# A four-layer decoder on one core: the k transfers issued by ScalarE, together with new stretch heads, half-wise waits, two-row moves of the maxima and new scheduler figures

## The reference

```python
q, k, v = x @ Wq + bq, kv @ Wk + bk, kv @ Wv + bv          # split in 16 heads of 8
w = softmax(q @ k.T * scale + mask, axis=-1)               # 512 x 512 or 512 x 77
y = layernorm(x + (w @ v) @ Wo + bo)
```

## Time and profile before

| what | value |
|---|---|
| median of 3 runs | 2757.01 us (2756.97 to 2764.75) |
| the profiled execution's own time | 2757.16 us |
| its span, first to last instruction | 2755.4 us |
| mean granted TensorE clock | 0.846 of full speed |
| first segment, first to last instruction | about 40 to 1104 us |
| second segment | about 1214 to 1790 us |
| third segment (L3c) | about 2291 to 2447 us |

### The profile page before, as it was taken

One profiled execution on the slowest core, in us unless ns is written; L12 is line 12 of the kernel. 1 busy time (PEld: TensorE's weight loads), 2 busy tenths in 40 slices (PEclk: granted clock), 3 DMA queues, 4 the chain that ended last, 5 costly groups with the idle time before them and its releaser, 6 DMA issues. The chain is left out here.

```text
span 2755.4 us, 44085 instructions
## 1 busy us (share of the span) xinstructions
PE 2173.7 (79%) x15402; PEld 1094.6 (40%) x15402; DVE 1629.0 (59%) x3578; ACT 1194.6 (43%) x2185; POOL 654.1 (24%) x845
## 2 busy tenths in 40 slices
PE   2699999975899996658999988629687773768888
PEld 1133355433233342634554444228422221335556
DVE  4588766577777732455676545235567772436666
ACT  0277756642267753223666675304232211433332
POOL 4211111134201110432121112044236673100000
PEclk9699999976589997777999998659888875779998
DMA  3300011100101010521111000038400001111111
GB/s 116 114 25 25 27 36 38 29 15 23 35 25 27 17 27 1 172 89 50 35 30 37 20 20 17 12 102 298 149 0 1 0 1 25 30 47 54 54 62 47
DMA packets 106846, 133.01 MB, mean 48 GB/s; under 512 B 26006, under 2 KB 90326, under 8 KB 105987
## 3 DMA queue, kind: packets, MB, share of 16 engines
q1 hardware_dynamic: 101556, 115.32, 14.0%
q0 software_dynamic: 3776, 7.79, 0.8%
q10 hardware_dynamic: 1296, 7.08, 0.7%
HBM read 70.65 MB, written 13.49 MB: 31 GB/s over the span
## 5 line engine op out<-in xcount | busy, mean ns | idle before, releaser
L1326 ACT ACTIVATE probs<-psE 128x512 f32<-128x512 f32 (+2 forms) x1248 | 698.0, 584 | 405.7 <-PE psE L1165 229.4
L1450 DVE TENSOR_REDUCE maxima<-psM 128x2 f32<-128x1024 f32 (+4 forms) x640 | 678.9, 1082 | 312.7 <-PE psM L1142 142.7
L1165 PE MATMUL psE<-q_stack,k_stack 53*128 53x512 bf16 (+3 forms) x1152 | 372.1, 361 | 36.6 <-ACT probs L1326 26.3
L1142 PE MATMUL psM<-k_stack,q_stack 51*128 51x512 bf16 (+3 forms) x1280 | 358.9, 352 | 32.2 <-DVE maxima L1450 13.9
L1601 POOL TENSOR_SCALAR pool_t<-mean_var 128x4 f32<-128x4 f32 x60 | 15.0, 250 | 935.7 <-DVE mean_var L1387 931.0
L2299 DVE SCALAR_TENSOR_TENSOR hres<-psM,gates,hres 128x128 f32<-128x128 f32 x512 | 144.2, 345 | 81.8 <-PE psM L2233 81.0
L1165 PEld LDWEIGHTS psE<-q_stack,k_stack 53*128 53x128 bf16 x1152 | 98.2, 94 | 229.2 <-ACT probs L1326 144.8
L1142 PEld LDWEIGHTS psM<-k_stack,q_stack 51*128 51x128 bf16 x1280 | 101.5, 96 | 196.2 <-issue 105.6
L1077 PE MATMUL psM<-masks_bf,ident_bf 64*128 64x128 bf16 (+2 forms) x832 | 148.3, 260 | 16.7 <-DMA k_stack<-k_parts 15.8
L2233 PEld LDWEIGHTS psM<-values,probs 128*128 128x128 f32 x1024 | 136.5, 195 | 59.4 <-issue 58.9
L1185 PE MATMUL psB<-probs,values 128*32 128x256 f32 (+3 forms) x1712 | 154.3, 432 | 2.4 <-ACT probs L1326 1.0
(11 more groups left out here) (411 smaller groups left out, 3614.4 us busy)
## 6 DMA issues: line engine op xcount, KB each, us to landing
q_stack<-q_parts SPq DMA_DIRECT2D x432, 64.0 KB
values<-experts_dram SPq DMA_DIRECT2D x40, 514.0 KB, 4.7
values<-experts_dram SPq DMA_DIRECT2D x32, 512.0 KB, 3.2
k_stack<-k_parts SPq DMA_DIRECT2D x192, 64.0 KB
hid<-experts_dram SPq DMA_DIRECT2D x15, 514.0 KB, 4.4
work<-experts_dram SPq DMA_DIRECT2D x15, 514.0 KB, 4.7
pack<-pack_dram SPq DMA_DIRECT2D x1, 4647.0 KB
work<-sorted SPq DMA_DIRECT2D x70, 65.0 KB, 3.7
```

The costliest lines, as they stand in the source:

```text
L1142: out, len(heads), keys, lo, max_mask(c, t), lambda i, to, start, stop: nc.tensor.matmul(to, q_stack[lo:lo + R_MAX, job.a % Q_SLOTS, pair_ ...
L1165: lambda h, to, start, stop: nc.tensor.matmul(to, ks[lo:lo + R_END, pairs[h], k * P:k * P + c.kn], q_stack[lo:lo + R_END, job.a % Q_SLOTS, ...
L1326: nc.scalar.activation(probs[0:c.kn, m % 2, heads[0]:heads[-1] + 1, q0:S], psE[0:c.kn, n % 2, 0:len(heads) * (S - q0)].rearrange("p (h q) ...
L1450: nc.vector.tensor_reduce(top, psM[:, at:at + len(banks), 0:per * keys].rearrange("p b (h k) -> p b h k", h=per), AX_X, ALU.max, negate=Tr ...
```

## The change

1. **Who issues k.** The 12 `k_move` transfers of every attention (and the bias rows of L2c) are issued from ScalarE's queue, in the order that the plan gives, between its exponentials and copies. q and the rows of maxima stay with SP.
2. **Halves.** The transfers go half by half: first the six of half 0, then the six of half 1, each half with semaphores of its own. A wide attention's sets 0 and 1 wait for half 0 alone, sets 2 and 3 for half 1. A narrow one still waits for both.
3. **Stretch heads.** For jobs marked `ahead` (L0a, L1a and L2s of sequence 0, L3c of all four) `k_split` runs on DVE instead of POOL.
4. **Rows of maxima.** The two bfloat16 parts lie together in `max_parts`, so one transfer writes both rows of a half: one issue for a wide set (two before), two for a narrow set (four before).
5. **Quantization.** The DVE task `quant_b` is cut in two, `quant_b` and `quant_c`, so that other work can be placed between; `peak` has one buffer for each sequence.
6. **Scheduler figures.** An issue is assumed to take 0.65 us of SP's or ACT's time (1.3 us for the two of a narrow set's rows) and to land 1.8 us after it; most DVE post-processing tasks are assumed a little shorter. With that the order on every engine changes.

The core of the diff (names of the places between @@ are added):

```diff
@@ Plan @@
             self.put(t + 8.0, "quant_b", job)
+            self.put(t + 12.0, "quant_c", job)
...
-            self.moved[n % 2] += 32 if c.wide else 64
+            self.moved[n % 2] += 16 if c.wide else 32
...
-            return [("q_move", m.job, 2 * NB - 1), ("k_move", m.job, 2 * NB - 1)] if m.g == 0 else []
+            if m.g not in (0, 2):
+                return []
+            last = NB - 1 if m.job.att.wide and m.g == 0 else 2 * NB - 1
+            return [("q_move", m.job, last), ("k_move", m.job, last)]
...
-        if task in ("q_move", "k_move"):
+        if task == "k_move":
+            return ("ACT",)
+        if task == "k_split":
+            return ("DVE",) if x.ahead else ("POOL",)
+        if task == "q_move":
...
-                    "quant_b": 9.5, "post_c": 1.75}[task]
+            return {"post_a": {"norm": 1.6, "mlp": 3.1}.get(x.post, 2.4) if task == "post_a" else 0.0,
+                    "post_b": {"twice": 2.8, "tail": 5.0}.get(x.post, 1.4) if task == "post_b" else 0.0,
+                    "q_evac": 0.8, "rq_evac": 2.3, "rk_evac": 2.3, "split": 0.5, "share": 0.7, "mix": 0.7, "quant_a": 1.7,
+                    "quant_b": 3.6, "quant_c": 4.0, "post_c": 1.4, "k_split": 2.2 if task != "k_split" or x.att.wide else 1.0}[task]
...
-            elif engine == "SP":
-                moves = task in ("q_move", "k_move")
-                n = 1 if moves else 2 if x.job.att.wide else 4
-                free[engine] = at + 0.06 * n
-                queue = max(queue, free[engine]) + (0.1 if not moves else 0.35 if task == "q_move" or x.att.wide else 0.08)
-                end = queue + 1.7
+            elif engine == "SP" or task == "k_move":
+                free[engine] = at + (1.3 if task == "rows_evac" and not x.job.att.wide else 0.65)
+                ended["ISSUED", item] = free[engine]
+                end = free[engine] + 1.8
...
@@ segment @@
+        def parts(me, engine, src, tmp, out, n):
+
+            me.mark(engine.tensor_copy(out[:, 0, 0:n], src[:, 0:n]))
+            me.wait()
+            me.mark(engine.tensor_tensor(tmp[:, 0:n], src[:, 0:n], out[:, 0, 0:n], ALU.subtract))
+            me.wait()
+            me.mark(engine.tensor_copy(out[:, 1, 0:n], tmp[:, 0:n]))
+            me.wait()
+            return engine.tensor_tensor(out[:, 2, 0:n], tmp[:, 0:n], out[:, 1, 0:n], ALU.subtract)
...
+                def wait_k_split(eng, job):
+
+                    if job.ahead:
+                        eng.wait_ge(k_split_ahead, split_no["k_split_ahead"][job])
+                    else:
+                        eng.wait_ge(k_split, split_no["k_split"][job])
+
+                def part_rows(j, hb):
+                    return slice(64 * hb + j, 64 * hb + NB * (DH - 1) + j + 1, NB)
+
+                def move_k(eng, job, i):
+
+                    hb, j = divmod(i, NB)
+                    nk = job.att.nk
+                    ks, _ = k_side(job)
+                    if i == 0:
+                        wait_k_split(eng, job)
+                        if before_k[job]:
+                            eng.wait_ge(exp_taken, job_exps(before_k[job]))
+                    if j == 0 and job in bias_rows:
+                        at = 64 * hb + R_BIAS
+                        src = job.att.bias if bias_rows[job] else zeros_bf[:, 0:nk]
+                        eng.dma_start(ks[at:at + 3, :, 0:nk], src.unsqueeze(1).to_broadcast([3, H // 2, nk]))\
+                            .then_inc(k_moved(job, hb), 16)
+                    eng.dma_start(ks[part_rows(j, hb), :, 0:nk],
+                                  k_parts[64 * hb:64 * hb + 64, (0, 1, 2, 0, 1, 0)[j], 0:nk])\
+                        .then_inc(k_moved(job, hb), 16)
...
-                            if m.g == 0 and step == 0 and b == 0:
-                                pe.wait_ge(q_moved[job.a % Q_SLOTS], q_need[job])
-                                pe.wait_ge(k_moved(job), k_need[job])
+                            if m.g in (0, 2) and step == 0 and b == 0:
+                                for hb in (m.g // 2,) if c.wide else (0, 1):
+                                    pe.wait_ge(q_moved[job.a % Q_SLOTS][hb], q_need[job])
+                                    pe.wait_ge(k_moved(job, hb), k_need[job])
...
@@ scalar queue @@
-                            since(act, k_split, evac_no["k_evac"][job] - 1)
+                            if job.a:
+                                wait_k_split(act, atts[job.a - 1])
...
+                        elif task == "k_move":
+                            move_k(act, job, item[2])
...
@@ vector queue @@
+                        elif task == "k_split":
+                            if job.att.rope:
+                                dve.wait_ge(k_roped, k_roped_no[job])
+                            else:
+                                wait_freed(dve, job, "k")
+                            if job.a:
+                                for hb in range(2):
+                                    dve.wait_ge(k_moved(atts[job.a - 1], hb), k_need[atts[job.a - 1]])
+                            splits += 1
+                            parts(me, nc.vector, k_full, q_tmp, k_parts, job.att.nk).then_inc(k_split_ahead, 1)
...
-                            high, low = max_parts[:, m.n % 2, :, 0:heads], max_parts[:, m.n % 2, :, heads:2 * heads]
-                            top = maxima[:, m.n % 2, :, 0:heads]
+                            n = min(heads, 8)
+                            split = max_parts[:, m.n % 2, :, 0:2 * heads].rearrange("p t (b two h) -> p t b two h", two=2, h=n)
+                            high, low = split[:, :, :, 0, :], split[:, :, :, 1, :]
+                            top = maxima[:, m.n % 2, :, 0:heads].rearrange("p t (b h) -> p t b h", h=n)
...
-                            quantize(me, u)
+                            quant_scale(me, u)
+                        elif task == "quant_c":
+                            quant_round(me, job.u)
...
@@ sync queue @@
-                            j, hb = divmod(i, 2)
-                            if i == 0:
+                            hb, j = divmod(item[2], NB)
+                            if item[2] == 0:
...
-                        elif task == "k_move":
-                            i, nk = item[2], job.att.nk
...
-                            for part in range(2):
-                                for hb in ((m.g // 2,) if c.wide else (0, 1)):
-                                    lo, p0 = 64 * hb + R_MAX + part, pair_of(HG * m.g) if c.wide else 0
-                                    n = min(heads, 8)
-                                    at = heads * part + (0 if c.wide else 8 * hb)
-                                    sp.dma_start(q_stack[lo:lo + 1, m.job.a % Q_SLOTS, p0:p0 + n, :],
-                                                 max_rows[at:at + n, m.n % 2, :]).then_inc(rows_moved[m.n % 2], 16)
-
-        def quantize(me, u):
+                            for hb in ((m.g // 2,) if c.wide else (0, 1)):
+                                lo, p0 = 64 * hb + R_MAX, pair_of(HG * m.g) if c.wide else 0
+                                at = 0 if c.wide else 16 * hb
+                                sp.dma_start(q_stack[lo:lo + 2, m.job.a % Q_SLOTS, p0:p0 + n, :],
+                                             max_rows[at:at + 2 * n, m.n % 2, :]).then_inc(rows_moved[m.n % 2], 16)
...
@@ segments @@
-            Job("att", u, L0a, "std", xt[:, u]),
+            Job("att", u, L0a, "std", xt[:, u], ahead=u == 0),
...
-            Job("att", u, L1a, "std", xt[:, u]),
+            Job("att", u, L1a, "std", xt[:, u], ahead=u == 0),
...
-            Job("att", u, L2s, "inner", yt[:, u], ("lnx_g", "lnx_b")),
+            Job("att", u, L2s, "inner", yt[:, u], ("lnx_g", "lnx_b"), ahead=u == 0),
...
-            Job("att", u, L3c, "std", xt[:, u]),
+            Job("att", u, L3c, "std", xt[:, u], ahead=True),
```

More of the change, by code:

```diff
@@ L425, in needs @@
             return [("root", x, 0)]
+        if task == "quant_c":
+            return [("quant_b", x)]
         if task == "post_b":
@@ L461, in engines @@
             return ("ACT",)
-        if task in ("q_evac", "rq_evac", "rk_evac", "split", "share", "mix", "quant_a", "quant_b", "post_a", "post_b",
+        if task in ("q_evac", "rq_evac", "rk_evac", "split", "share", "mix", "quant_a", "quant_b", "quant_c", "post_a", "post_b",
                     "post_c"):
@@ L1407, in _ @@
                     nc.vector.memset(values[:, :, :, :, DH:DH + 1], 1.0)
+                    splits = 0
                     for item in plan.order["DVE"]:
@@ L1573, in _ @@
                             if q_before:
-                                pool.wait_ge(q_moved[q_before.a % Q_SLOTS], q_need[q_before])
+                                for hb in range(2):
+                                    pool.wait_ge(q_moved[q_before.a % Q_SLOTS][hb], q_need[q_before])
                                 pool.wait_ge(q_split, split_no["q_split"][job] - 1)
```

108 lines of the change are left out of this document (46 added, 62 removed).

## The result

The changed kernel takes 2881.5 us in the median of four runs (2866.2 to 2889.0), the kernel before 2757.0 us: 1.044 times as long, 95% interval 1.039 to 1.049. The forecast was 2708 us. The profiled execution after took 2866.2 us with a span of 2864.4.

The account below looks back on a forecast made before the run. TensorE was taken as the bound in the wide-attention stretches, VectorE from 552 to 690 us. The terms -11.5 - 12 - 5 - 26.5 - 4 + 10 = -49 us took 2757.2 to 2708 us, range 2670 to 2765.

Parts of the forecast that it names:

- What bounds the kernel: TensorE in the wide-attention stretches, 396.5 of 414 us and 264.2 of 275; VectorE leads from 552 to 690 us.
- ScalarE's price: Cost of moving k and bias issues to ScalarE: +10 us, between 0 and 100, most issues standing alone.
- first rival: ScalarE becomes the bound: overdue k transfers in a row stop exponentials and TensorE in wide attentions; 2798 us, chance 0.13.
- The upper bound: Twelve issues in a row: some 6 us of TensorE in each of 17 wide attentions, 100 us.
- The price of single issues: One issue between two exponentials on ScalarE costs some 0.1 us, nothing where ScalarE waits for TensorE.
- The heads: First score matmuls at stretch starts come sooner through halves and two queues: L0a -11.5 us, L2s -12.
- two queues are no faster: Rival: transfers themselves are the limit, so heads gain less and L3c's period nothing; 2743 us, chance 0.10.
- L3c: Last narrow attentions: head -10, first maxima rows -1.4, period from 28.5 to 21 to 26 us, -15; in all -26.5.
- The -10 of the head: L3c's first attention: q alone on SP lands at 2308.2 instead of 2318.3 us.
- Scheduler figures: New issue and duration figures, changing the order on every engine: 0 us, with -10 to +20.
- L1a: Sequence 0's head starts sooner, though VectorE is the bound there: -5 us, bounds 0 and -12.
- rows of maxima: Outside L3c, fewer issues per set shorten TensorE's waits for them: -4 us, 0 to -8.

Follow-up runs that it names:

- e13: e11 with its order kept, plus twelve small transfers nobody waits for, issued in a row from ScalarE in each wide attention; +229 us against 2675.9 us.
- e11: e1 with the old durations of VectorE's tasks and the new model of SP's queue; 2676 us.
- e1: The changed kernel with the k transfers of every attention issued from SP again, all else kept; 2693 us, ratio 0.976.
- e12: The changed kernel with k's transfers due no earlier than the planned end of the last exponential that reads their slot; 2754 us.
- e15: e11 plus twelve small transfers nobody waits for per wide attention, issued from ScalarE singly behind twelve successive exponentials; +23 us against 2675.9 us.
- e2: The kernel before with only the k transfers moved to ScalarE's queue, under the old model of transfers; 2777 us, ratio 1.009.
- e8: e1 with the split of k given back to GpSimd everywhere; 2709 us.
- e6: e1 with the old durations of VectorE's tasks and the old model of SP's queue; last stretch 460 us, whole time not stated.
- e3: The changed kernel with the planner allowing the next k transfer only 0.3 us after the last is issued; 2802 us.
- e17: e12 with e11's durations of VectorE's tasks; 2795 us.

## Why the prediction was wrong

**What bounds the kernel** was right: e13 stalls ScalarE, which is busy only 45% of e11's span, and the time follows because TensorE, in the wide stretches, goes idle.

**The step that failed** is ScalarE's price: "the plan may take a ready transfer in any such gap, so most will stand alone. [...] I take +10". 188 us were paid (e1). Two things in it were wrong.

First, the premise on the order. The prediction's own first rival named the condition, "where k's parts are late, the transfers are overdue and come in a row", and gave it 0.13. It is the slot that is late, not k's parts, and that could be read in the plan: with two slots k waits for the last exponential of the attention two before, while its due times lie earlier. e12 moves nothing but these and gets 128 us back.

Second, the price of a row. The upper bound was 6 us for each wide attention: 7.8 us of issues less two exponentials in flight. Measured by itself a row costs 11.5 us (e13). TensorE's idle time was bounded about rightly (6.7 us for each row); the clock was left out, which stood at its lower level for 9.7 us behind the row shown and costs 5.0 us for each. With 11.5 in place of 6 the rival's sum gives 2757 - 59 + 17 x 11.5 = 2894 us, near the 2881 measured. By the twelve wide rows that the trace has, they are 138 of the 188 us (an estimate from e13), which fits the 128 that e12 gets back; the rest are the rows of narrow attentions, single and short groups of issues, and the order, not separated.

The price of single issues was right: 0.1 us each was said, 0.1 measured (e15), 20 us for all issues of k (e2). (The count was 8 too high: the trace has 8 bias rows, 440 issues in all.)

**The heads** were right for TensorE's first scores. L0a -10.5 (forecast -11.5, at 66.0 us and not 65), L2s -11.3 (-12). Counted from the stretch's start L3c's first scores came 9.1 us sooner (-10). But the second queue gives only part of it. With all of k on SP (e1) the three still start 7.6, 7.9 and 4.0 us sooner than before, so the second queue adds 2.9, 3.4 and 5.1. In L0a and L2s that leaves most to the halves and the order of issues, since e8 shows nothing for the split; the two were not tested apart. Here the rival "two queues are no faster" was wrong: an issue takes 0.70 us in place of 0.61 while both issue, and twelve on each queue are through in 9.6 us. In L0a, VectorE's first cast of the split took 1.19 us (from 55.27) beside GpSimd's subtraction, which ended at 56.19; the second, alone, took 0.43. The parts were ready at 58.4 all the same, the early end of the forecast.

**L3c** came out at -20.5 in all, and -26.1 with k on SP; -26.5 was forecast. That this is near is luck, for the terms were not right. The -10 of the head never reached the exponentials: the first came 5.5 us later than before. The period from one attention's first exponential to the next fell by 8.3 us on average (27.7 to 19.4), where 5 were forecast, and in e1, without the second queue, by 10.6. I gave the period to the second queue and the figures nothing. e6 has every other edit and a last stretch of 460 us, e11 437: the planner's new model of the queue makes 23 of the 26. And e2, with k on ScalarE but the old model, has 465. The reading that q and k "occupy SP" for the 22.7 us from 2322.1 to 2344.8 was wrong too: 24 issues of 0.65 us are 15.6 of it, the rest is rows of maxima and pauses.

**Scheduler figures** "0, with -10 to +20" was wrong in that place, and elsewhere within what a nudge does (13 us in all, 19 in a stretch). **L1a** and **rows of maxima** were not tested apart. All parts but the queue were forecast at -59 and measured at -64 (e1). That agreement is luck as well: the forecast took head and L3c gains from a second queue that e1 does not have, and e1's first stretch shrank by 44 us where -16.5 was forecast for its two heads, while the second grew by 4 where -12 was forecast. Where the 44 us come from is open.

**What stays open.** Between e12 (2754 us) and e1 lie 61 us. Single issues explain 20 to 24. e3, e12 and e17 show that an order with k on ScalarE can land at 2754 or 2795 us without the rows of the changed kernel. In both e3 and e17 the first stretch holds the loss, and most of it is busy time at the lower clock (59 of 87 us and 91 of 92). In e3 half clock is seen behind an alternation that e15 survives at the upper clock, but whether k's arrival, the order of the projections or the two together let TensorE idle there was not separated. No version with all of k on ScalarE came below 2754.

## What to carry to other kernels

In this kernel transfers issued from a computing engine were nearly free while they stood singly, each beside an operation, and ten times as dear in a row; before moving them, look in the plan for what makes them become ready together (a slot that comes free late, due times already past). The price of a stall of TensorE, where it is the bound, was the stall and the stretch at the lower clock behind it. A sum that comes out right can hide terms that are wrong: compare it term by term. And where an order is planned, nudge a figure once: what the nudge does to the time is the least that another variant has to show. Of these kernels e11 beats both, at 2676 us (0.971, interval 0.967 to 0.974), with all of k on SP.

## What the runs showed of the hardware

- An issue of ScalarE's queue runs beside the operation ahead of it (0.02 us after its start, 0.68 long in e15) and holds up the next one by 0.2 us. A row of eleven or twelve holds it up for 7.6 (e13) to 9.9 us (346.8 us of the changed kernel, where SP issues too).
- The lower clock outlasts the stall: 6.76 us of idle TensorE were followed by 9.7 us at 0.50 (e13), 1 us lost of 7 by 20 us (e3). In e17 it lasts from 120 to 260 us at 0.52, with TensorE busy 95%.
- Two queues that issue at the same time slow each other a little: 0.70 us an issue in place of 0.61.
- VectorE's cast of 128x512 from float32 to bfloat16 took 0.43 us alone and 1.19 beside a subtraction on GpSimd (the changed kernel, 57.23 and 55.27 us).
